# Cross attention in a decoder layer: the query projection per row tile of 128 columns instead of per chunk of 512, and a pipeline of two steps fewer

## The reference

```python
x = x + self_attention(layernorm(x), ...)        # random features, 16 heads
def cross_attention(x, y, Wq, bq, Wk, bk, Wv, bv, Wo, bo):   # 8 heads of 32
    q = x @ Wq + bq; k = y @ Wk + bk; v = y @ Wv + bv
    weight = softmax(einsum('bhqd,bhkd->bhqk', q, k) / sqrt(32))
    return einsum('bhqk,bhkd->bhqd', weight, v) @ Wo + bo
x = x + cross_attention(layernorm(x), ctx, ...)
x = x + expert_attention(layernorm(x), ...)      # 8 heads, 8 experts
```

## Time and profile before

| what | value |
|---|---|
| median of 3 runs | 985.78 us (984.88 to 988.14) |
| the profiled execution | 985.28 us |
| its span, first to last instruction | 983.5 us |
| mean granted TensorE clock | 0.995 |
| busy: PE, DVE, ACT, POOL | 95%, 69%, 40%, 24% |

### The profile page before, as it was taken

The page is one execution under the profiler, slowest core; times in us unless marked ns, Lnnn a source line. Parts: engine busy times, 40 slices in busy tenths (PEclk is TensorE's granted clock), DMA queues, the critical chain, the costliest instruction groups (busy, mean ns, idle before and its releaser), DMA issues.

```text
span 983.5 us, 14697 instructions
## 1 busy us (share of the span) xinstructions
PE 937.1 (95%) x5620; PEld 728.7 (74%) x5620; DVE 682.3 (69%) x1054; ACT 390.1 (40%) x680; POOL 236.3 (24%) x253
## 2 busy tenths in 40 slices
PE   5989999999998999999999998999999999999997
PEld 3568778887655565799976785888876656569997
DVE  3767666547555877898858575765574777879886
ACT  3634555130465757400124355630205655751000
POOL 6212412222532303135620032300032101411000
PEclk9999999999999999999999999999999999999999
DMA  7003000333144422156630000023120000023663
GB/s 256 26 23 129 2 1 1 135 129 129 65 150 158 165 85 65 44 177 177 181 130 1 1 2 0 2 66 113 52 86 35 23 22 0 25 73 108 184 198 100
DMA packets 33739, 81.56 MB, mean 83 GB/s; under 512 B 5847, under 2 KB 10551, under 8 KB 33671
## 3 DMA queue, kind: packets, MB, share of 16 engines
q1 hardware_dynamic: 32391, 76.44, 23.9%
q10 hardware_dynamic: 1280, 4.20, 1.5%
HBM read 61.26 MB, written 19.20 MB: 82 GB/s over the span
## 4 chain that ended last, share of the span: by engine, by line
PE 77%; DVE 10%; ACT 4%; DMA 4%; issue 3%; POOL 1%; SPq 0%; ACTq 0%; DVEq 0%; POOLq 0%
PE ps L1090 18%; PE ps L1396 10%; PE ps L1333 7%; PE ps L1401 5%; PE ps L1248 5%; PE ps L1293 5%; PE ps L1098 4%; PE ps L1309 3%; PE ps L1200 3%; PE ps L1262 3%; DVE region L984 3%; PE ps L1215 2%; PE ps L1369 2%; PE ps L1370 2%; DMA expert<-in_output_experts 2%
## 5 line engine op out<-in xcount | busy, mean ns | idle before, releaser
L1333 PE MATMUL ps<-region 128*128 128x512 f32 (+3 forms) x384 | 161.5, 504 | 0.0
L963 DVE TENSOR_REDUCE region<-ps 128x1 f32<-128x512 f32 (+1 forms) x192 | 98.1, 551 | 67.2 <-PE ps L1312 67.2
L744 ACT ACTIVATE region<-ps 128x512 f32<-128x512 f32 x192 | 92.2, 486 | 121.5 <-PE ps L1372 109.4
L1008 DVE COPY_PREDICATED region<-region,ps 128x512 f32<-128x512 uint32 x112 | 82.0, 736 | 72.0 <-PE ps L1090 71.4
L1396 PE MATMUL ps<-expert_hi,kst 128*128 128x256 f32 x512 | 124.3, 283 | 3.3 <-DVE kst L1038 2.3
L1396 PE MATMUL ps<-expert_lo,kst 128*128 128x256 f32 x512 | 122.5, 279 | 0.0
L1090 PE MATMUL ps<-expert_hi,wide_hi 128*128 128x512 f32 x256 | 102.7, 401 | 0.0
L1090 PE MATMUL ps<-expert_hi,wide_lo 128*128 128x512 f32 x256 | 100.2, 392 | 0.0
L1090 PE MATMUL ps<-expert_lo,wide_hi 128*128 128x512 f32 x256 | 99.9, 390 | 0.0
L1396 PEld LDWEIGHTS ps<-expert_hi,kst 128*128 128x128 f32 x512 | 96.4, 188 | 4.5 <-DVE kst L1038 2.7
L543 ACT ACTIVATE region<-ps 64x512 f32<-64x512 f32 (+4 forms) x146 | 80.8, 556 | 47.1 <-PE ps L1215 20.0
(11 more groups left out here) (148 smaller groups left out, 1780.2 us busy)
## 6 DMA issues: line engine op xcount, KB each, us to landing
region<-hot_rows SPq DMA_DIRECT2D x128, 128.0 KB, 3.4
expert_hi<-halves_kept SPq DMA_DIRECT2D x24, 512.0 KB, 3.6
expert_lo<-halves_kept SPq DMA_DIRECT2D x24, 512.0 KB, 4.8
halves_kept<-expert_hi SPq DMA_DIRECT2D x16, 512.0 KB, 2.6
halves_kept<-expert_lo SPq DMA_DIRECT2D x16, 512.0 KB, 3.9
expert<-in_value_experts SPq DMA_DIRECT2D x8, 512.0 KB, 5.1
expert<-in_output_experts SPq DMA_DIRECT2D x8, 512.0 KB, 5.0
gb<-gate_rows ACTq DMA_DIRECT2D x16, 256.0 KB, 3.8
```

The source lines that it names most:

```text
L744: act.activation(PT[:, g % RING, lo:CH], ps[:, 4 + g % 2, 0:CH - lo], ACT.Exp).then_inc(sem["pt_ready"], 1)
L963: dve.tensor_reduce(mx[:, i, at_mx:at_mx + 1], ps[:, max_bank(h, m), 0:w], AX.X, ALU.max).then_inc(sem["s_max"], 1)
L1008: dve.copy_predicated(V3_heads[:, t], chosen.unsqueeze(3).broadcast_to([P, PAIRS3, 2, HD3]), ps[:, n % 4, :].rearrange("p (a i k) -> p a i ...
L1333: mm(ps[:, SUM_BANK[c], lo:CH], V3[:, j, h // 2, h % 2 * HD3:(h % 2 + 2) * HD3], PT[:, g % RING, lo:CH], start=(j == 0), stop=(j == TC * ( ...
```

## The change

The query projection of cross attention is made for every row tile, in the step in which its X is: 2 halves of 128 columns, 2 matmuls for each, both halves into bank 2 (columns 0 to 127 and 128 to 255), with one semaphore step for the tile. ACT evacuates the halves with two ACTIVATEs of 128 columns. X moves from behind Y to ahead of C in PE's program; the projection stays behind Y. F waits in every step from 7 on for the queries of the step before (q2_sb up to s - 6), whether it works for self or cross attention, since the projection writes its bank. The projection waits for f_sub of its own step and for xT of its tile. OFFSET becomes (0, 8), so cross attention starts two steps earlier, LAST is 25, and the step numbers of the value experts and gates follow.

```diff
--- before.py
+++ after.py
@@ -186,7 +186,7 @@
             n_ps=2, n_sb=1, nT_ps=1, n_blk=6, za_ps=1, n_ready=3,
             f_ps=2 * TT, top_ready=2 * TT * DA, f_sub=2 * TT, f_exp=2 * TT, fT_ps=2 * TT, fT_sb=2 * TT,
             num_ps=2 * TT, cx_ready=2 * TT, cxT_ps=2 * TT, cxT_sb=2 * TT, y_ps=2 * TT,
-            q2_ps=2 * NC, q2_sb=2 * NC,
+            q2_ps=TT, q2_sb=TT,
             gate_ps=NC, gate_exp=NC, g_ready=NC, gT_ps=1, gT_a=1,
             val_ps=TT * E3, val_a=TT, val_v=TT * (E3 - 1), v3_ready=TT + 1,
             qk_ps=PAIRS3 * 2 * NC, qk_sb=PAIRS3 * 2 * NC,
@@ -241,7 +241,7 @@
 
         SQUARES_AT = {1: range(0, 2), 2: range(2, 6), 5: range(6, 10), 6: range(10, 14), 7: range(14, 16)}
         QUERIES_AT = {3: (0,), 4: (1,), 7: (2, 3)}
-        OFFSET = (0, 10)
+        OFFSET = (0, TT)
         VALUES_AT = OFFSET[1] + TT + 1
         LAST = VALUES_AT + TT
         GATES_AT, GATE_BANK = (VALUES_AT + 2, VALUES_AT + 5), (6, 5)
@@ -664,9 +664,12 @@
                         norm_apply(b, a + 1, t)
                     for a, t in due(s, 6):
                         norm_evac(b, a + 1, t)
-                        if a == 0 and t % TC == TC - 1:
-                            for n in range(2 * (t // TC), 2 * (t // TC) + 2):
-                                biased(kqT, n, 2, 4, "q2_ps", "q2_sb", b)
+                        if a == 0:
+                            until(act, "q2_ps", b, t + 1)
+                            for half in range(DA):
+                                last = act.activation(kqT[:, half, t * P:(t + 1) * P], ps[:, 2, half * P:(half + 1) * P],
+                                                      ACT.Identity, bias=cols[:, 4 + half:5 + half])
+                            last.then_inc(sem["q2_sb"], 1)
                     if s in GATES_AT:
                         gates(GATES_AT.index(s))
                     if 0 <= (t := s - VALUES_AT) < TT:
@@ -1186,10 +1189,10 @@
                 for s in range(LAST):
                     for a, t in due(s, 0):
 
+                        until(pe, "q2_sb", b, min(TT, max(0, s - 6)))
                         if a == 0:
                             until(pe, "q_sb", b, 2 * (t // TC + 1))
                         else:
-                            until(pe, "q2_sb", b, 2 * (t // TC + 1) if s <= TT + 5 else 2 * NC)
                             if t == 0:
                                 pe.wait_ge(v2_placed, 16 * len(V2_RUNS))
                         until(pe, "f_sub", b, a * TT + t)
@@ -1248,6 +1251,8 @@
                             last = mm(ps[:, 6, w0:w0 + w], phT[0:r, t % 2, k * P:(k + 1) * P], src,
                                       start=(k == 0), stop=(k == chunks - 1), skip_group_check=True)
                         last.then_inc(sem["num_ps"], 1)
+                    for a, t in due(s, 6):
+                        norm_transpose(b, a + 1, t)
                     for a, t in due(s, 3):
                         until(pe, "cx_ready", b, a * TT + t + 1)
                         until(pe, "cxT_sb", b, a * TT + t)
@@ -1263,15 +1268,16 @@
                                       start=(i == 0), stop=(i == DA - 1))
                         last.then_inc(sem["y_ps"], 1)
                     for a, t in due(s, 6):
-                        norm_transpose(b, a + 1, t)
-                        if a == 0 and t % TC == TC - 1:
+                        if a == 0:
 
                             until(pe, "xT_ready", b, TT + t + 1)
-                            until(pe, "f_sub", b, TT + max(0, s - OFFSET[1] + 1))
-                            for n in range(2 * (t // TC), 2 * (t // TC) + 2):
-                                if n >= 2:
-                                    until(pe, "q2_sb", b, n - 1)
-                                projection(n, 2, W2q, "q2_ps")
+                            until(pe, "f_sub", b, s + 1)
+                            until(pe, "q2_sb", b, t)
+                            for half in range(DA):
+                                for i in range(DA):
+                                    last = mm(ps[:, 2, half * P:(half + 1) * P], W2q[:, i, half * P:(half + 1) * P],
+                                              xT[:, i, t * P:(t + 1) * P], start=(i == 0), stop=(i == DA - 1))
+                            last.then_inc(sem["q2_ps"], 1)
                     if s in GATES_AT:
                         gates(GATES_AT.index(s))
                     if 0 <= (t := s - VALUES_AT) < TT:
```

## The result

The changed kernel takes 1001.53 us (median of 4, 1001.39 to 1001.72), against 985.33 us (median of 4, 983.24 to 988.14) before: a ratio of 1.0163 with a 95% interval of 1.014 to 1.0187, so it is slower by 1.6%, clear of the spread. Its profiled execution has a span of 999.9 us, 16.4 more than before.

The account below looks back on a forecast made before the run. PE, busy 95% of the span, bounds the kernel. Projection work and two new stalls, 19.46 us a batch against 11.12 before, add 16.7 for two batches to 985.3: 1002 us forecast, range 993 to 1007.

Parts of the forecast that it names:

- PE's work the same: Query projection's matmuls on PE: 7.10 us a batch before, 7.04 after, the same within 0.1 us.
- Stall A: New wait of the query projection for xT in each of eight steps, behind ACT's queue: 4.66 us a batch.
- Stall B: New wait of the next step's features for the queries' evacuation from bank 2: 0.97 us a step, 7.76 a batch.
- the pair: A tile's two 128-column evacuations on ACT: 0.73 us together, the second starting 0.37 after the first.
- The sum: Projection work and stalls: 19.46 us a batch after, 11.12 before; net +8.34 a batch, +16.7 for two.
- What is hidden: ACT's some 2.9 us more evacuation work a batch adds no separate delay; DVE, GpSimd and DMA cause none.
- F's wait for DVE's subtraction: Sign: this wait of 0.54 us at the start of cross attention is gone.
- the last sign: The first product of the value experts starts about 8.3 us later in batch 0.
- The two steps: Loop of 25 steps instead of 27: worth at most PE's old stalls, 4.02 us a batch, going only with them.
- rival 1: Short projections hide, old stalls go, no new ones appear: 4.08 us a batch won, 977 us; chance 4%.
- Rival 2: ACT makes xT in time, only the wait for the queries' evacuation remains: 993 us, half hidden 997; chance 12%.
- Rival 3: PE's clock falls in the new steps' stalls: 1005 us with one spell a batch, 1024 in every step; chance 7%.

Follow-up runs that it names:

- e3: Changed kernel with the query projection in bank 7 and one step later, between the feature transposes and the numerators: 976.13 us.
- e5: Changed kernel with the query projection in bank 7 and xT copied first on ACT, projection still in its own step: 975.19 us.
- e1: Changed kernel with the query projection written into the free half of bank 7 instead of bank 2: 990.13 us.
- e2: Changed kernel with the copy into xT moved ahead of the context transposes' copy and the normalisation in ACT's program: 989.13 us.
- e7: Changed kernel with the transposes of the normalised rows back behind the output projection on PE, the query projection behind them: 1000.17 us.
- e6: Changed kernel with one copy of 256 columns in place of the two evacuations, the queries' bias left out: 998.01 us.
- e4: Changed kernel with OFFSET (0, 10) as before, the projection per tile staying in bank 2: 1010.12 us.
- e8: Changed kernel with the projection in bank 7 and one step later, and OFFSET (0, 10): 982.86 us.

## Why the prediction was right

The forecast was 1002 us, slower, and 1001.5 was measured. Term by term, per batch:

- **PE's work the same:** right where N stands behind Q: e3 has 0.89 us a tile, 0.88 forecast. With F behind it, as in the changed kernel, it is 0.99 to 1.08 (e5, e1). In the changed kernel Q takes longer from its start to ACT's (1.20 us, forecast 0.88 + 0.16 + 0.04 = 1.08), where its input has only just arrived; in step 8 of e5, where it is older, it takes 1.10. This was not in the sum.
- **Stall A, 4.66:** measured 0.78 + 0.77 + 0.53 + 0.52 + 4 x 0.61 = 5.0 in starts. Steps 6 to 9 are as forecast; in steps 10 to 13 the exponential of cross attention holds ACT 0.09 us longer, which I had left out. e2 shows that the cause is ACT's order, e7 that moving X forward is worth nothing.
- **Stall B, 7.76:** the step from Q's start to F's was forecast as 0.88 + 0.97 = 1.85 and is 1.87. That it fits so well is luck: two sizes in it were off and cancelled, the pair, which took 0.62 and not 0.73, and Q's start to ACT's, 0.12 more. The eight small evacuations of line 592 were the wrong neighbour: they don't overlap, these do, by 0.11 us (2 x 0.364 - 0.62). Here the Trainium skill, "ScalarE: Activation LUTs", section "What ACT_TABLE_LOAD costs", was nearer with its overlap of some 93 ns; the estimate by its formula for 128 columns, 387 ns, is 23 above the measured 364. e1 shows the stall, e6 its rate.
- **The sum:** net +8.34 a batch forecast, +8.65 measured; the rest of the program gave 0.9 back, which is no effect of the change, since the front, where the programs are the same, moved by 0.83. So the loops took 17.3 us more and not 16.7, and that the total comes within 0.5 us of the forecast is partly luck. The measured terms themselves add up to 5.04 + 8 x 1.87 - 11.12 = 8.9 a batch, some 0.2 more than the loop; that rest is not traced.
- **What is hidden:** ACT's extra work was put at 2.9 us a batch; by the forecast's own 0.36 and 0.69 it is 16 x 0.36 - 4 x 0.69 = 3.0. Nothing rests on it. Of the signs named, that of the pair misses, since its second evacuation starts 0.26 and not 0.37 us after the first. F's wait for DVE's subtraction is gone, as forecast, and the last sign holds too: the first product of the value experts starts at 157.21 us instead of 149.51, 7.7 later, or 8.5 counted from F of step 6, against 8.3 forecast.
- **The two steps:** the weak point. "The two steps are worth at most those, and they go only with the stalls" held for the size: e3 against before wins 3.5 of the 4.02. But I took a thin step to cost only the 0.54 of one wait for DVE. e4 and e8 show 3.1 to 3.6 and 2.5 us a loop, and e8 that 1.0 of e3's 3.5 goes without the two steps. The forecast did not need this number, since it took the old stalls from the trace.
- **The rivals:** rival 1 (the short projections hide) is false for the changed kernel, and e3 and e5 show what it takes: 976 and 975 us against its 977. Rival 2 (A hidden) is false, 16 waits. Rival 3 (the clock falls) is false here:

```profile
100.00:120.00 20.00, 16.51 (x132) 14.26 (x133) 10.02 (x26) 10.38 (x22) 4.66 (x12) 1.00 0.00 1
120.00:140.00 20.00, 16.51 (x134) 13.94 (x131) 10.93 (x30) 9.76 (x25) 6.02 (x13) 1.00 0.01 2
```

PE is busy for 16.5 of 20 us and the granted clock stays at 1.00, as in the rest of both loops. The mechanism exists, though: in e4 it fell in both batches behind the hole of 2.06 us. A thin stretch alone did not do it: from 132 to 136 us of e4 PE was busy for 2.03 of 4 us, with holes of 1.25 and 0.72 us, and the clock stayed at 1.00 there and behind.

## What to carry to other kernels

Cutting a block into smaller ones to shorten a pipeline multiplies every handover at its borders: count the borders that one block had, the borders that the pieces have, and what each engine has to do in between. Two questions decide: does the next block in the queue write the bank that is just being emptied, and what stands ahead of the input's last copy in the queue of the engine that makes it? Where both can be answered by a free bank and an order, as in e5, the same cut turns from 1.6% slower into 0.9% faster.

## What was not expected

The eight records of Q have a pace of 0.11 us, but what follows Q starts 1.08 us after it in e1, 0.99 in the later steps of e5 (107.58 to 108.57) and 0.89 in e3, where N and not F is next. So some 0.10 us go with an input that has only just come (the group's record is then 1.16 us, otherwise 1.05 or 1.06; in step 10 of e8 it is 1.16 with a copy that ended 0.34 us before Q, in step 8 of e5 1.05 with one that ended 0.50 before), and some 0.10 with F, whose matmuls use 64 of the 128 rows, standing next. The kernel before has the second part at the end of its steps too: Y's share is 0.96 where F follows it (from 90.10 to 91.06, in the changed kernel from 89.27 to 90.23) and 0.87 where another block does. Neither was in the forecast. What they are in the engine the records don't say.

The length of the loop repeats to 0.02 us between the batches of most executions (e4, with its clock falls, is the exception), while the stretch between the loops, whose program is the same in all these kernels, took from 400.7 us (e5) to 405.6 (e1). Part of this spread is where the clock falls: in e1 the granted clock was 0.89 from 300 to 310 us, 0.94 from 310 to 320 and 0.83 from 560 to 570, by estimate (the missing share times 10 us) up to 1.1, 0.6 and 1.7 us of the 4.9; in e5 it did not fall between the loops. The same happens ahead of the loops. In the self-attention queries, in front of any change, the same stretch of the program ran at 0.50 of the clock in the execution before and at 1.00 in the one after:

```profile
38.00:40.00 2.00, 2.00 (x6) 0.51 (x5) 0.00 (x0) 0.49 (x1) 0.00 (x0) 0.50 0.19 78
```

```profile
38.00:40.00 2.00, 2.00 (x10) 0.94 (x10) 0.00 (x0) 1.01 (x2) 0.00 (x0) 1.00 0.53 211
```
